# A second set of buffers for the rotation's products, and ScalarE in place of SyncE issuing the row swaps

## The reference

```
q, k, v = x @ Wq, x @ Wk, x @ Wv          # 16 heads of 64, 8 sequences of 512 tokens
q, k = rope(q), rope(k)                   # pairs of neighbouring channels are rotated
attn = softmax(where(causal, q @ k.T / 8, -inf))
x1 = layernorm(x + (attn @ v) @ Wo + bo)
w = top-2 of softmax(x1 @ gate.T + bias)  # 8 experts, weights normalised to sum 1
f = sum over the 2 experts e of w_e * gelu(x1 @ up_e.T) @ down_e.T
out = layernorm(x1 + layernorm(f) + x1)   # the inner norm and sum are the FFN's own
```

## Time and profile before

| | |
|---|---|
| median of 3 runs | 814.8 us |
| the profiled execution's own time | 816.16 us |
| its span in the trace | 814.4 us |
| mean granted TensorE clock | 0.982 |
| TensorE matmul busy | 766.8 us, 94% |
| VectorE busy | 602.2 us, 74% |
| ScalarE busy | 563.7 us, 69% |
| GpSimd busy | 573.0 us, 70% |
| DMA queue q1 (SP's) | 147.73 MB, 59.0% of the 16 engines' time |
| DMA queue q10 (ScalarE's) | 1.17 MB, 1.0% |

### The profile page before, as it was taken

One profiled execution on the slowest core, in us unless ns is written; L12 is line 12 of the kernel. 1 busy time (PEld: TensorE's weight loads), 2 busy tenths in 40 slices (PEclk: granted clock), 3 DMA queues, 4 the chain that ended last, 5 costly groups with the idle time before them and its releaser, 6 DMA issues.

```text
span 814.4 us, 19400 instructions
## 1 busy us (share of the span) xinstructions
PE 766.8 (94%) x5259; PEld 548.5 (67%) x5259; DVE 602.2 (74%) x2144; ACT 563.7 (69%) x1616; POOL 573.0 (70%) x701
## 2 busy tenths in 40 slices
PE   8999999999999999999999999979998899999995
PEld 4555566666766566666666666656665579999995
DVE  6667677888798768978896688668876855225996
ACT  4577777777778767877677667756776656555676
POOL 4576767558776867696669776946686356999993
PEclk9899999999999999999999999999999999999998
DMA  4677778666866676767675756555568767434525
GB/s 145 192 238 222 220 230 246 212 214 207 249 194 222 194 207 198 221 213 219 205 224 177 221 171 217 185 181 190 193 195 235 234 195 204 118 85 126 161 86 159
DMA packets 146793, 158.85 MB, mean 195 GB/s; under 512 B 23616, under 2 KB 122432, under 8 KB 146688
## 3 DMA queue, kind: packets, MB, share of 16 engines
q1 hardware_dynamic: 133248, 147.73, 59.0%
q0 software_dynamic: 4224, 8.72, 3.3%
q10 hardware_dynamic: 9216, 1.17, 1.0%
HBM read 74.66 MB, written 46.20 MB: 148 GB/s over the span
## 4 chain that ended last, share of the span: by engine, by line
PE 65%; issue 8%; DVE 7%; DMA 7%; POOL 7%; SPq 4%; ACT 1%; DVEq 0%; ACTq 0%; POOLq 0%
PE AO L1158 12%; PE S_all L1119 9%; PE S_all L1327 7%; PE S_all L1138 6%; PE AO L1177 5%; PE AO L1340 3%; PE TB L1340 3%; DMA hT<-norms 3%; PE TB L1138 2%; DMA turns<-turned_pr 2%; PE TB L1119 2%; SPq L469 1%; PE AO L1054 1%; PE AO L1056 1%; SPq L621 1%
## 5 line engine op out<-in xcount | busy, mean ns | idle before, releaser
L1446 ACT ACTIVATE Pr_all<-Sm,nmax 128x512 f32<-128x512 f32 (+3 forms) x512 | 280.6, 554 | 89.0 <-DVE nmax L1684 88.5
L773 POOL TENSOR_TENSOR qk<-shared,qk 128x512 f32<-128x512 f32 x64 | 82.0, 1281 | 144.9 <-DMA qk<-shared 135.4
L1684 DVE CUSTOM_DVE_ANT_0 Sm<-S_all,causal 128x512 f32<-128x512 f32 (+2 forms) x384 | 170.8, 507 | 2.5 <-PE S_all L1119 2.3
L1158 PE MATMUL AO<-PT,shared 128*64 128x128 f32 x1008 | 153.9, 448 | 12.1 <-issue 10.1
L1119 PEld LDWEIGHTS S_all<-qk 64*128 64x128 f32 x768 | 69.8, 188 | 102.8 <-issue 86.6
L1119 PE MATMUL S_all<-qk 64*128 64x512 f32 (+2 forms) x768 | 129.5, 469 | 1.1 <-issue 1.0
L1158 PEld LDWEIGHTS AO<-PT,shared 128*64 128x64 f32 x1008 | 66.4, 139 | 62.2 <-issue 46.6
L1456 ACT ACTIVATE PT<-S_all 128x768 f32<-128x768 f32 (+1 forms) x129 | 70.1, 596 | 41.1 <-PE S_all L1138 41.1
L1446 ACT ACTIVATION_READ_ACCUMULATOR Pr_all<-Sm,nmax 128x1 f32 x512 | 98.3, 192 | 0.0
L847 POOL DMA_INDIRECT xrows<-pay,slot x64 | 65.6, 1025 | 33.7 <-issue 17.2
L1645 DVE TENSOR_TENSOR shared<-TB,cos_t 128x512 f32<-128x512 f32 x62 | 42.9, 691 | 61.8 <-PE TB L1056 31.0
(11 more groups left out here) (342 smaller groups left out, 1708.1 us busy)
## 6 DMA issues: line engine op xcount, KB each, us to landing
turns<-turned_pr SPq DMA_DIRECT2D x63, 512.0 KB
PT<-turns SPq DMA_DIRECT2D x252, 128.0 KB, 3.0
qk<-shared SPq DMA_DIRECT2D x124, 256.0 KB
hT<-norms SPq DMA_DIRECT2D x110, 128.0 KB
PT<-yrows SPq DMA_DIRECT2D x7, 512.0 KB, 4.2
w_tile<-in_wup SPq DMA_DIRECT2D x10, 256.0 KB, 3.3
xt<-xrows SPq DMA_DIRECT2D x32, 65.0 KB, 3.2
x_acc<-in_x SPq DMA_DIRECT2D x8, 256.0 KB, 3.9
```

The source lines that it names most:

```text
L773: nc.gpsimd.tensor_tensor(qT[p][:, :], q_cos, qT[p][:, :], ALU.add).then_inc(q_ready, 1)
L1158: last = nc.tensor.matmul(to, V[u // VS % 2][:, kb, u % VS * P + D * h:u % VS * P + D * h + D], pt_rows(p, h, kb), start=(kb == QB - 1), s ...
L1446: nc.scalar.activation(Pr[j][:, 0:n], Sm[j], ACT.Exp, bias=nmax[:, j:j + 1], scale=-1.0, accum_out=rsum[p][:, h * QB + qb:h * QB + qb + 1] ...
L1684: nc.vector.tensor_tensor_reduce(out=Sm[j], in0=score_bank(group, h)[:, at:at + n], in1=causal[:, T - n:T], scale=-0.125, scalar=HUGE, op0 ...
```

## The change

There are now two of each product buffer, used by even and odd units. The second set lies in memory that becomes `xt` and `xT` once attention is over, so the first load of an expert's rows waits for the last rotations. `rope_q` of unit u waits for rotate_q of unit u-2, not u-1. The two swap DMAs leave SP's program and are issued by ScalarE right behind store_norms, one unit later in its program: in unit u ScalarE swaps unit u+1, under the same three waits as before. SP goes straight from store_turned(u) to load_turned(u).

```diff
-        q_cos, q_rot, k_rot, k_even = (turning[:, i, :] for i in range(4))
-        qk_rot = turning[:, 1:3, :]
+        k_even = turning[:, 3, :]
+        xt_first = sb("xt_first", [P, 8 * ROW])
+        xT_all = sb("xT_all", [P, 4 * P])
+        q_cos = [turning[:, 0, :], xT_all[:, :]]
+        qk_rot = [turning[:, 1:3, :], xt_first[:, 0:2 * T].rearrange("p (i t) -> p i t", t=T)]
+        q_rot, k_rot = ([qk_rot[i][:, which, :] for i in range(2)] for which in range(2))
@@ SyncE, each unit
                 if not last:
                     store_turned(u, p)
-                if first:
-                    load_turned(u, p)
-                if u + 2 < UNITS:
-                    swap(u + 2, p)
-                if not first and not last:
+                if not last:
                     load_turned(u, p)
@@ SyncE, load_rows
+                if t == 0:
+                    sp.wait_ge(q_ready, UNITS)
+                    sp.wait_ge(k_ready, UNITS)
@@ GpSimd
-                nc.gpsimd.tensor_tensor(qT[p][:, :], q_cos, qT[p][:, :], ALU.add).then_inc(q_ready, 1)
+                nc.gpsimd.tensor_tensor(qT[p][:, :], q_cos[p], qT[p][:, :], ALU.add).then_inc(q_ready, 1)
-                nc.gpsimd.tensor_tensor(k_rot, k_cos[u % 2], sin_t[:, :], ALU.mult)
+                nc.gpsimd.tensor_tensor(k_rot[u % 2], k_cos[u % 2], sin_t[:, :], ALU.mult)
@@ ScalarE, each unit
                     store_norms(u - 1, 1 - p)
+                    if PLAIN <= u + 1 < UNITS:
+                        swap(u + 1, 1 - p)
...
+            def swap(u, p):
+                act.wait_ge(k_read, u + 1)
+                act.wait_ge(q_read, u + 1)
+                act.wait_ge(scored, BLK * (u - 1))
+                nc.scalar.dma_start(qk[p][0:P:2, :, :], qk_rot[p][1:P:2, :, :]).then_inc(swapped, 16)
+                nc.scalar.dma_start(qk[p][1:P:2, :, :], qk_rot[p][0:P:2, :, :]).then_inc(swapped, 16)
@@ VectorE, rope_q
-                wait(dve, q_ready, u)
+                wait(dve, q_ready, u - 1)
                 bank = q_bank(u)
-                nc.vector.tensor_tensor(q_cos, bank[:, :], cos_t[:, :], ALU.mult)
-                nc.vector.tensor_tensor(q_rot, bank[:, :], sin_t[:, :], ALU.mult).then_inc(q_read, 1)
+                nc.vector.tensor_tensor(q_cos[u % 2], bank[:, :], cos_t[:, :], ALU.mult)
+                nc.vector.tensor_tensor(q_rot[u % 2], bank[:, :], sin_t[:, :], ALU.mult).then_inc(q_read, 1)
```

More of the change, by code:

```diff
@@ L252, in build_block @@
         wdown = sb("wdown", [P, E * IB, C])
-        xt = [sb(f"xt{i}", [P, ROW])[:, :] for i in range(8)]
+        xt = [xt_first[:, i * ROW:i * ROW + ROW] for i in range(8)]
         v_old, v_old_more = shared[:, 0:T], shared[:, T:2 * T]
         xt += [t[:, i * ROW:i * ROW + ROW] for t in (cos_t, sin_t, qT[1], v_old) for i in range(3)]
-        xT = [sb(f"xT{i}", [P, P]) for i in range(4)]
+        xT = [xT_all[:, i * P:i * P + P] for i in range(4)]
         w_tile = [sb(f"w_tile{i}", [P, I]) for i in range(2)] + [qT[0], kT[0]]
@@ L599, in load_norms @@
                                  rows.rearrange("a q r -> a (q r)").unsqueeze(0).to_broadcast([D, LANES, P])).then_inc(norms_in, 16)
-            def swap(u, p):
-                sp.wait_ge(k_read, u + 1)
-                sp.wait_ge(q_read, u + 1)
-                wait(sp, scored, BLK * (u - 1))
-                sp.dma_start(qk[p][0:P:2, :, :], qk_rot[1:P:2, :, :]).then_inc(swapped, 16)
-                sp.dma_start(qk[p][1:P:2, :, :], qk_rot[0:P:2, :, :]).then_inc(swapped, 16)
             def store_turned(u, p):
@@ L1028, in space @@
                 wait(pool, spaced, spaces[0])
-                nc.gpsimd.memset(k_rot[:, 0:SPACE], 0.0).then_inc(spaced, 1)
+                nc.gpsimd.memset(k_rot[0][:, 0:SPACE], 0.0).then_inc(spaced, 1)
                 spaces[0] += 1
@@ L1641, in rope_q @@
                 dve.wait_ge(q_proj, u + 1)
-                wait(dve, q_ready, u)
+                wait(dve, q_ready, u - 1)
                 bank = q_bank(u)
-                nc.vector.tensor_tensor(q_cos, bank[:, :], cos_t[:, :], ALU.mult)
-                nc.vector.tensor_tensor(q_rot, bank[:, :], sin_t[:, :], ALU.mult).then_inc(q_read, 1)
+                nc.vector.tensor_tensor(q_cos[u % 2], bank[:, :], cos_t[:, :], ALU.mult)
+                nc.vector.tensor_tensor(q_rot[u % 2], bank[:, :], sin_t[:, :], ALU.mult).then_inc(q_read, 1)
                 if u < PLAIN:
                     dve.wait_ge(q_read, u + 1)
-                    nc.vector.stream_shuffle(qT[u % 2], q_rot, swap).then_inc(swapped, SWAPPED)
+                    nc.vector.stream_shuffle(qT[u % 2], q_rot[u % 2], swap).then_inc(swapped, SWAPPED)
             def second_k():
@@ L1654, in second_k @@
                 nc.vector.tensor_tensor(k_cos[1], bank[:, :], cos_t[:, :], ALU.mult)
-                nc.vector.tensor_tensor(k_rot, bank[:, :], sin_t[:, :], ALU.mult).then_inc(k_read, 1)
+                nc.vector.tensor_tensor(k_rot[1], bank[:, :], sin_t[:, :], ALU.mult).then_inc(k_read, 1)
                 dve.wait_ge(k_read, 2)
-                nc.vector.stream_shuffle(kT[1], k_rot, swap).then_inc(swapped, SWAPPED)
+                nc.vector.stream_shuffle(kT[1], k_rot[1], swap).then_inc(swapped, SWAPPED)
             def turn(u, h):
@@ L1669, in first_k @@
                 nc.vector.tensor_tensor(k_cos[0], SB[2][:, :], cos_t[:, :], ALU.mult)
-                nc.vector.tensor_tensor(k_rot, SB[2][:, :], sin_t[:, :], ALU.mult).then_inc(k_read, 1)
+                nc.vector.tensor_tensor(k_rot[0], SB[2][:, :], sin_t[:, :], ALU.mult).then_inc(k_read, 1)
                 dve.wait_ge(k_read, 1)
-                nc.vector.stream_shuffle(kT[0], k_rot, swap).then_inc(swapped, SWAPPED)
+                nc.vector.stream_shuffle(kT[0], k_rot[0], swap).then_inc(swapped, SWAPPED)
                 dve.wait_ge(swapped, 2 * SWAPPED)
```

## The result

The changed kernel took 855.3 us (median of 4 runs, 851.87 to 860.07) beside 815.4 us of the kernel before on the same chip: ratio 1.0465, 95% interval 1.0423 to 1.0507. It is slower, as forecast, but by 40 us, not by 7, and outside the range. The profiled execution took 851.87 us, span 850.1, mean granted clock 0.987 (before 0.982), so the clock is not the cause.

A forecast was written before the change was run, and what follows sets the result against it. TensorE's own work, 9.15 us a quiet unit, was taken as the bound, with stalls costing 51 us. Terms -7 + 8 + 5 + 1 = +7 on 816.16 gave 823.2, forecast as 822 because that execution was 1.4 above the median; range 804 to 837.

The forecast's parts named there:

- a rival with 0.15: Rival, chance 0.15: norms, swap, rotation and scores become one ring in each unit; 0.35 us a unit, 836 us.
- SP without the swap: SP's turned loads follow as soon as their store has landed; -7 us, ends -15 and 0.
- The brake that I saw in L1207: In unit 27, TensorE's transpose of rows GpSimd finishes at 282.49 is not earlier, so not all the loads' gain comes through.
- VectorE, 0: VectorE's 21.5 us of waits for rotate_q go, but nothing is counted beyond the freed loads' gain; end -4.
- The later swap: Swap issued behind the norms on ScalarE, 2.35 us later; scores late in four heavy units; +8 us, ends 2 and 14.
- So a quiet unit just holds: In quiet units the swap's 2.35 us of lateness fits the 2.48 us of slack before the scores, leaving 0.13.
- Transfers that meet: The swap now runs beside the turned loads on the same DMA engines, delaying attend; +5 us, ends 0 and +20.
- ScalarE's own time: The swap's two issues on ScalarE start its exponential 0.97 us later, mostly recovered; +1 us, ends 0 and +6.
- Just covered: ScalarE's two exponentials end at 313.3, and VectorE's turn, which needs the first, starts at 313.31.
- The ring: Rival, chance 0.15: norms, swap, rotation and scores, 9.02 us against 9.15, close into one loop each unit; 836 us.
- the third term: The swap's later issue behind the norms on ScalarE, making scores late in heavy units; +8 us.
- the fifth: The time ScalarE itself loses to the swap's two issues ahead of its exponentials; +1 us.

The follow-up runs named there:

- e3: The changed kernel with ScalarE issuing the swap ahead of store_norms, not behind it; 819.3 us, 1.0028 of the kernel before.
- e1: The changed kernel with the swap back on SyncE between store and loads, keeping two buffers and the looser rope_q wait; 819.1 us, ratio 1.0033.
- e20: e3 with two small, unneeded 16 KB DMAs behind the norms on ScalarE; 825.4 us, 1.0131 of the kernel before.
- e12: e3 with ScalarE waiting, ahead of the swap, for VectorE's second transpose of the reciprocal sums (`inverted`); 915.1 us, 1.1170 of the kernel before.
- e16: The changed kernel with the norms' DMA on SyncE ahead of the loads reading it back, and ScalarE's swap waiting for `inverted`; 980.8 us, ratio 1.2015.
- e5: The kernel before with `k_read` set by GpSimd's sine product, not the cosine product behind it; 807.3 us, ratio 0.9860.
- e8: e1 with `k_read` set by GpSimd's sine product, not the cosine product behind it; 808.1 us, 0.9868 of the kernel before.
- e7: The changed kernel with the swap issued by SyncE behind the loads; 870.3 us, 1.0621 of the kernel before.

## Why the prediction was wrong

The sign was right, the mechanism was in it, as a rival with 0.15, and the size was not. The terms in their order:

- **SP without the swap, -7.** The loads did come free: held 0.42 us behind their store's landing before, 0.02 now. But e3, with the same freedom and an early swap, is no faster than e1 (1.0028 and 1.0033). So it is 0 net of what ScalarE's two issues cost in e3, which was not separated. Part of why: the loads, now beside the swap, took 5.09 us from issue to landing in e3 and 4.94 before (medians). The three units 28, 45 and 61 did get 8.6 us shorter in the changed kernel, but in e3 only 3.8, and its unit 29 took such a stall instead. The brake that I saw in L1207 was none: it ended 1.98 us before attend in the earlier trace rows.
- **VectorE, 0.** Right: its wait left the view, and e1 shows no gain.
- **The later swap, +8: the step that failed.** It says "So a quiet unit just holds", with 9.02 us against 9.15, and puts the quiet units at nothing. The 23 units that took under 9.5 us before went from 9.17 to 10.10 us in the mean, 21.6 of the 34.8 us by which these 59 units grew. The heavy units that it priced at 8.4 us, those ended by the scores of 27, 43, 51 and 59, grew by 7.4: that part was right. In the 23 quiet ones the terms now measure: swap at S + 2.71 (2.12 in my sum), landing 4.03 (4.36), rotations 2.90 (2.54), and 0.47 to the scores (0): 10.11. Unit 30 was no lucky pick (before, the mean of the 23 is 1.63 for the norms, 4.37 for the landing and 2.55 for the slack; in unit 30 it is 1.79, 4.36 and 2.48), but a margin of 0.13 us is none when the landing alone goes from 2.9 to 6.8 us from unit to unit, and the sum left out 0.1 us each ahead of the swap and of the scores. Two pieces I left at their old times although they hang on the loop: VectorE's event (the norms at 2.05 in these 23 and not 1.63), and turn_k, which follows rotate_k and, when the slack is gone, ends at S + 2.4 and holds the swap itself (19 units). So the ring closes in 11 of the 23 quiet units and in 18 of the other 36, not in four.
- **Transfers that meet, +5.** The effect is there, and its size here is open. Issued within 0.7 us of the loads the swap took 5.48 us to land and the loads 6.45, otherwise 4.26 and 4.46, but that is so in 5 units of the changed kernel, since its loads go 2.4 us ahead of the swap. Over all units the landing took 4.36 us after, 4.17 before. e3 can't price it, because its 2.7 us of slack hide a longer landing. The Trainium skill ("DMA: Bandwidth & Descriptors", section "Issuing engines are not separate DMA queues") says that a second issuing engine saves the issue time alone; e3 against e1 agrees, since the queue of ScalarE brought no time.
- **ScalarE's own time, +1.** e20 prices it at about 8 us. "Just covered" was read from one unit.
- **The ring, 836 at 0.15.** Its arithmetic was right, its trigger ("as soon as ... the norms come after S + 1.9") was met by the mean of the kernel before, S + 2.05, which I had not taken; and its price of 0.35 us a unit was 0.59.

So most of the loss is the third term (20 us by TensorE's waits, up to 28 by subtraction), and at least part of the rest the fifth. What stays open, besides that split: the norms' event and the norms' DMA in front of the swap were not told apart by a run (e12 and e16 also held something else), though in all 59 units the norms go within 0.1 us of the event and the DMA itself holds the swap by some 0.4 us more.

## What to carry to other kernels

A DMA moved to a busy engine inherits every wait in front of it in that engine's order; write down what each instruction ahead waits for, and add the loop up unit by unit, taking in each the longer of the loop and the old unit, not once for a quiet unit and not with means either. With the means of all units before (norms 2.05, then 0.43 to the swap, landing 4.17, rotations 3.02, 0.10 to the scores) the loop is 9.77 us and seems to fit in 10.03. Added up in each of the 59 units it is longer than the unit in 25, by 26 us in all: an estimate from the trace before, with the 0.43 from the one after, and much nearer to the 34.8 measured. If several loops of nearly one length run through the same queues, an order that has its instructions in the time at which they become ready (swap, then norms) is worth more than the choice of the engine: two calls exchanged were worth 36 us, the engine nothing. And look at which product an event really needs: signalling one instruction sooner took 1.4% off, because it removed three idle stretches around which TensorE ran at half clock (the time is measured, the cause is read from the traces of e5 and e8).

## What was not expected of the hardware

After TensorE had idled 1.98 us ahead of attend in the earlier trace rows, its granted clock fell to 0.50, the lower of its two levels, for 3.4 us, and attend took 3.61 us in place of 2.37; a cause 1.1 us long cost 3.05 us. Two small DMAs' issues on ScalarE, which move next to nothing, took 0.97 us together (median) and about 1% of the kernel's time. The landing of the 512 KB swap depended little on who issued it, 4.12 us in the mean from SyncE between store and loads (e1), 4.40 from ScalarE (e3), 4.03 from SyncE behind the loads (e7), and much on what was issued beside it: 5.39 us within 0.7 us of the loads, 3.87 otherwise (e12), and the loads 6.46 and 4.85.
